# Seven block products instead of eight for two pairs of token groups: a gate projection on one core of Trainium2

## The reference

```python
def act_qdq(x):        # one scale for the whole tensor, 16 bits
    scale = max(max(abs(x)) / 32767, 1e-12)
    return clip(round(x / scale), -32768, 32767) * scale
# lpbq_dequant(w): 4-bit rounding with a scale for each block of 32 weights
x = act_qdq(layernorm(x2))
up   = act_qdq(x @ lpbq_dequant(w_up).T)      # w_up, w_gate: 1536 x 512
gate = act_qdq(x @ lpbq_dequant(w_gate).T)
gate = act_qdq(gate * fixed_qdq_u16(sigmoid(gate)))
out  = x2 + act_qdq(gate * up) @ lpbq_dequant(w_down).T
```

## Time and profile before

| | |
|---|---|
| Median of 3 runs | 889.84 us (888.32 to 889.88) |
| The profiled execution | 889.12 us, span of its instructions 887.3 us |
| TensorE matmul | 858.3 us busy, 97% of the span, 4108 matmuls |
| VectorE | 689.5 us busy, 78% |
| ScalarE | 585.5 us busy, 66% |
| GpSimd | 195.4 us busy, 22% |
| Granted TensorE clock, mean | 0.994 |

### The profile page before, as it was taken

One profiled execution on the slowest core, in us unless ns is written; L12 is line 12 of the kernel. 1 busy time (PEld: TensorE's weight loads), 2 busy tenths in 40 slices (PEclk: granted clock), 3 DMA queues, 4 the chain that ended last, 5 costly groups with the idle time before them and its releaser, 6 DMA issues.

```text
span 887.3 us, 11953 instructions
## 1 busy us (share of the span) xinstructions
PE 858.3 (97%) x4108; PEld 424.5 (48%) x4108; DVE 689.5 (78%) x965; ACT 585.5 (66%) x712; POOL 195.4 (22%) x170
## 2 busy tenths in 40 slices
PE   7999969999999999999999999999899989999998
PEld 5877544444444444444444444444444434444443
DVE  4879885566647459689998987584999997999892
ACT  2468776785655366599999987752889965455430
POOL 0099948399300295000000000000000000000000
PEclk9999989999999999999999999999999999999999
DMA  9822228766989549999779964997998887989872
GB/s 348 339 84 109 107 83 288 232 169 188 304 252 313 196 156 238 270 379 371 261 258 341 334 236 161 357 378 262 323 406 271 277 319 273 374 299 401 316 294 96
DMA packets 118402, 236.56 MB, mean 267 GB/s; under 512 B 47952, under 2 KB 57168, under 8 KB 116304
## 3 DMA queue, kind: packets, MB, share of 16 engines
q1 hardware_dynamic: 117200, 231.77, 74.0%
q10 hardware_dynamic: 1152, 4.19, 1.2%
HBM read 130.55 MB, written 95.42 MB: 255 GB/s over the span
## 4 chain that ended last, share of the span: by engine, by line
PE 71%; DVE 9%; POOL 8%; issue 6%; DMA 3%; SPq 1%; ACT 1%; DVEq 0%; ACTq 0%; POOLq 0%
PE ps L1106 28%; PE ps L1043 21%; PE ps L1159 13%; PE ps L1059 4%; PE ps L1186 4%; DVE big L1960 3%; DVE big L1953 3%; POOL big L875 2%; DMA big<-in_L_ffn_w_gate_dram 2%; POOL big L832 1%; POOL big L826 1%; PE ps L1176 1%; POOL small L872 1%; DMA big<-up_park 1%; POOL big L830 1%
## 5 line engine op out<-in xcount | busy, mean ns | idle before, releaser
L1106 PE MATMUL ps<-big 128*128 (+1 forms) x1152 | 248.8, 379 | 0.0
L1204 ACT ACTIVATE big<-ps 128x1024 f32<-128x1024 f32 (+2 forms) x154 | 126.4, 830 | 147.7 <-PE ps L1043 62.5
L1043 PE MATMUL ps<-big 128*128 (+1 forms) x864 | 186.6, 379 | 0.7 <-DVE big L1736 0.7
L1106 PEld LDWEIGHTS ps<-big 128*128 128x128 f16 x1152 | 112.7, 98 | 135.9
L1043 PEld LDWEIGHTS ps<-big 128*128 128x128 f16 x864 | 84.4, 98 | 102.7 <-issue 0.9
L1159 PE MATMUL ps<-big 128*128 128x512 f16 x576 | 125.1, 379 | 3.2 <-DVE big L1981 3.2
L817 POOL PARTITION_ALL_REDUCE small<-small x8 | 2.9, 368 | 451.6 <-DVE small L1922 170.1
L1781 DVE TENSOR_REDUCE small<-big 128x1 f32<-128x1024 f32 x36 | 43.8, 1218 | 71.0 <-ACT big L1204 71.0
L1159 PEld LDWEIGHTS ps<-big 128*128 128x128 f16 x576 | 56.2, 98 | 71.6 <-issue 2.9
L1140 PE MATMUL ps<-big 128*128 128x512 f16 x384 | 84.2, 379 | 4.3 <-ACT big L1489 4.3
L1874 DVE TENSOR_REDUCE small<-big 128x1 f32<-128x1024 f32 x48 | 58.2, 1215 | 13.7 <-ACT big L1204 13.6
(11 more groups left out here) (118 smaller groups left out, 1222.3 us busy)
## 6 DMA issues: line engine op xcount, KB each, us to landing
big<-up_park SPq DMA_DIRECT2D x90, 512.0 KB, 6.7
big<-gate_park SPq DMA_DIRECT2D x48, 512.0 KB, 6.3
up_park<-big SPq DMA_DIRECT2D x48, 512.0 KB, 4.1
gate_park<-big SPq DMA_DIRECT2D x36, 512.0 KB, 2.7
sign_park<-big SPq DMA_DIRECT2D x36, 256.0 KB, 2.7
big<-in_x_dram SPq DMA_DIRECT2D x8, 1024.0 KB, 18.5
x_park<-big SPq DMA_DIRECT2D x8, 1024.0 KB, 3.9
product_park<-big SPq DMA_DIRECT2D x16, 512.0 KB, 3.5
```

Source lines behind the costliest of these rows:

```text
L1043: mm = nc.tensor.matmul(unit_banks(n)[:, j], WG[:, x, a, k % 2, o:o + P], XT[:, g, b, k], start=(k == 0 and a + b == 0), stop=(k == KC - 1 ...
L1106: mm = nc.tensor.matmul(ps[:, b + j], WU[:, a, t // 3, k, t % 3], XT[:, g, c, k], start=(k == 0 and a + c == 0), stop=(k == KC - 1 and c = ...
L1204: return nc.scalar.activation(dst, src, ACT.Copy)
```

## The change

Groups 4 and 5 are taken as a second pair. There are 24 flat units and 12 quads; quads 0 to 5 take groups 6 and 7, quads 6 to 11 take groups 4 and 5. The differences of groups 4 and 5 are made at units 11 to 13 (and kept where the one pair's were), those of groups 6 and 7 at units 18 to 20, in another place. What lay on units 24 to 35 moves: the down weights' pieces to units 14, 16, 19 and 21, with new waits; the loads of the up weights to quads 0 and 1, behind the last store of down weights; their block maxima to quads 1 to 4, scales to quads 4 and 5; their pieces to quads 7 to 10. At the end SP fetches five gate tiles in a row, since their stores ended six quads earlier.

```diff
-FLAT_G = 6
+FLAT_G = 4
 FLAT = FLAT_G * UPG
-QUADS = UPG
+PAIRS = (NG - FLAT_G) // 2
+QUADS = PAIRS * UPG
-DOWN_AT = (14, 17, 20, 23)
-PARK_AT = (16, 19, 22, 25)
-TURN_AT = 25
-UP_AT = (0, 1, 2, 3)
-LOAD_AT = 26
-BLOCKS_AT = (28, 29)
-SCALE_AT = (30, 32)
+DOWN_AT = (14, 16, 19, 21)
+PARK_AT = (17, 19, 22, 24)
+TURN_AT = (19, 12)
+UP_AT = (7, 8, 9, 10)
...
+        def pair_group(pr):
+            return FLAT_G + 2 * (PAIRS - 1 - pr)
+
+        def turns(pr):
+            t = part(HT0 + 4 * UW, 4096) if pr else part(U0, 4096)
...
+                    if g == 6:
+                        sp.wait_ge(t_raw, T_RAW + 4)
...
+                if q == 0:
+                    park_down_weights(KC - 1)
+                if q < 2:
+                    load_up_weights(2 * q)
+                    load_up_weights(2 * q + 1)
+                if q == UP_AT[0] + 1:
+                    sp.wait_ge(q_mm, Q_MM + done_p7(UPG * (PAIRS - 1) - 1))
+                    sp.wait_ge(t_lo, T_LO + 4 * PAIRS)
...
-            fetch_late_gate(1)
-            fetch_late_gate(2)
             for x in (2, 3):
                 park_half(QUADS - 1, x)
-            fetch_late_gate(3)
-            fetch_late_gate(4)
...
+            for x in (1, 3):
+                sp.wait_ge(c_st[x], C_ST + 16 * UPG)
+            for i in range(1, 6):
                 fetch_gate(i)
...
-                    pe.wait_ge(t_lo, T_LO + 4)
+                    pe.wait_ge(t_lo, T_LO + 4 * PAIRS)
...
+                else:
+                    act.wait_ge(t_lo, T_LO + 4)
...
+                act.wait_ge(t_raw, T_RAW + (count if pr or j < 2 else 8))
+                if pr == 0 and j == 0:
+                    h_turned(act, NG - 1)
...
+                elif pr == 0:
+                    dve.wait_ge(t_lo, T_LO + 4)
+                    dve.wait_ge(wd_turned, 32)
                 if j == 0:
-                    dve.wait_ge(wd_turned, 32)
                     h_turned(dve, g)
                     h_turned(dve, g + 1)
...
+                if 1 <= q < 5:
+                    up_block_max(q - 1)
+                if q == 4:
+                    block_scales(1)
+                if q == 5:
+                    common_scale(1, 3)
                 half_max(q, 0)
```

More of the change, by code:

```diff
@@ L240, in whole_sum @@
             return part((4 + x) * 2048, 1536)
-        T = part(HT0 + 4 * UW, 4096).bitcast(F16).rearrange("p (j l k t) -> p j l k t", j=4, l=2, k=2)
+        def pair_group(pr):
+            return FLAT_G + 2 * (PAIRS - 1 - pr)
+        def turns(pr):
+            t = part(HT0 + 4 * UW, 4096) if pr else part(U0, 4096)
+            return t.bitcast(F16).rearrange("p (j l k t) -> p j l k t", j=4, l=2, k=2)
         raw_sum = part(U0 + 4096, 2048).rearrange("p (s w) -> p s w", s=2)
@@ L594, in _ @@
             fetch_gate(7)
+            for x in (2, 3):
+                park_half_sign(QUADS - 1, x)
             def next_gates(n):
@@ L1063, in first_of @@
             def first_of(q, base):
-                g = FLAT_G
-                six(base + 1, q, WG[:, 1], XT[:, g, :, 2:4], True)
+                g = pair_group(q // UPG)
+                six(base + 1, q % UPG, WG[:, 1], XT[:, g, :, 2:4], True)
             def quad(q):
-                base, g, n = 4 * ((q + 1) % 2), FLAT_G, q
+                base, pr, n = 4 * ((q + 1) % 2), q // UPG, q % UPG
+                g, T = pair_group(pr), turns(pr)
                 need(pe, c_ev, C_EV + 4 * (q - 1) if q > 1 else 0)
@@ L1361, in _ @@
                 nc.scalar.activation(sign_out[:, u % 2], gate_out[u % 3], ACT.Sign).then_inc(sign_ev, 1)
-                for j in range(4):
-                    if u == TURN_AT + j // 2:
-                        turn_hi(j)
+                for pr in range(PAIRS):
+                    for j in range(4):
+                        if u == TURN_AT[pr] + j // 2:
+                            turn_hi(pr, j)
                 if u % 2 and u < 2 * NG - 3:
@@ L1771, in turn_raw, with turn_lo @@
                                         ALU.add if j == 2 else ALU.subtract).then_inc(t_raw, 1)
-            def turn_lo(j):
-                dve.wait_ge(t_hi, T_HI + j + 1)
-                hi, lo = (T[:, j, l].rearrange("p k t -> p (k t)") for l in range(2))
+            def turn_lo(pr, j):
+                dve.wait_ge(t_hi, T_HI + (j + 1 if pr else 4 + j + 1))
+                hi, lo = (turns(pr)[:, j, l].rearrange("p k t -> p (k t)") for l in range(2))
                 nc.vector.scalar_tensor_tensor(lo, raw_sum[:, j % 2], 0.25, hi, ALU.mult,
@@ L1796, in _ @@
                     sum_lo(SUM_AT.index(u))
-                if u == TURN_AT - 1:
-                    turn_raw(0)
-                    turn_raw(1)
-                if u == TURN_AT:
-                    turn_lo(0)
-                    turn_lo(1)
-                    turn_raw(2)
-                    turn_raw(3)
-                if u == TURN_AT + 1:
-                    turn_lo(2)
-                    turn_lo(3)
-                if u in BLOCKS_AT:
-                    up_block_max(2 * BLOCKS_AT.index(u))
-                    up_block_max(2 * BLOCKS_AT.index(u) + 1)
-                if u == SCALE_AT[0]:
-                    block_scales(1)
-                if u == SCALE_AT[1]:
-                    common_scale(1, 3)
+                for pr in range(PAIRS):
+                    if u == TURN_AT[pr] - 1:
+                        turn_raw(pr, 0)
+                        turn_raw(pr, 1)
+                    if u == TURN_AT[pr]:
+                        turn_lo(pr, 0)
+                        turn_lo(pr, 1)
+                        turn_raw(pr, 2)
+                        turn_raw(pr, 3)
+                    if u == TURN_AT[pr] + 1:
+                        turn_lo(pr, 2)
+                        turn_lo(pr, 3)
                 for c in range(OC):
```

27 lines of the change are left out of this document (8 added, 19 removed).

## The result

The changed kernel takes **896.18 us** (median of 5 runs, 894.04 to 897.33); the kernel before, on the same chip, 889.88 us (5 runs, 888.32 to 890.70). The ratio is 1.0071, with a 95% interval of 1.0053 to 1.0090: 6.3 us slower, where 887.3 was forecast. The profiled execution of the changed kernel took 896.1 us, with a span of 894.3; before it was 889.12 and 887.3.

The account below looks back on a forecast made before the run. TensorE was taken to set the stage's end: -7.8 for matmuls removed, +1.1 and +2.4 flat-stage stalls, +0.3 and +1.5 hand-over, sum -2.5, giving 887.3 us by the median of 889.84. Range 883.6 to 891.6; the forecast's own 885.5 to 889.0.

Parts of the forecast that it names:

- the size of the pair's operations: Flat stage, units 11 to 13: the second pair's VectorE operations beside GpSimd take 1.5 us each, bounds 1.2 and 2.1.
- the lock rival: Flat stage: each of the second pair's eight operations waits a whole GpSimd instruction, chain 3.6 later; 890.9 us, chance 0.13.
- 0.3 for another wait: Hand-over to quads: first half store lands at 271.5, about when quad 1's first combination wants its buffer; 0.3 us lost.
- the forecast's own upper end for the flat part: Flat stage and quad 0's second product: at most 7 us lost, with the second pair's eight operations at 2.1 each.
- the hand-over's 1.5: Quad 1: combine(2, 0) ends at 283.0 behind load and block maximum, TensorE wants it at 281.6; 1.5 us, bounds 0 and 8.
- the late loads rival: Quad 1: up-weight load lands 12 us after issue, VectorE waits at up_block_max(0) before combine(1, 1); 893.7 us, chance 0.12.
- the natural pieces in quads 7 to 10: Quads 7 to 10: they cost TensorE 0.4 us as in quads 0 to 3, nothing net, bounds -0.4 and +0.8.
- GpSimd's pieces for the up weights: Late quads: all eight pieces end at about 353, quad 10 asks for the last at 355; hidden by 2 us.
- the block maxima and scales in quads 3 to 5: Quads: a 1.75 us maximum fits VectorE's 2.71 gap; quad 4's scales make combine(4, 1) 1.7 late, recovered; no cost.
- the last up transposes: End of the quads: issued in quad 11, landing at 371.9 before ScalarE's first scaling at 373; hidden by 1 us.
- the differences in units 11 to 13 take 2 us each: Sign against the forecast: with up products starting after 371, these long flat-stage operations would point to the lock rival.
- quad 1 holds the gap: Sign against the forecast: with up products starting after 371, a gap there would point to the late loads rival.

Follow-up runs that it names:

- the kernel with both causes away: Changed kernel with the third natural_hi's wait shortened, first two down-piece sets at units 15 and 17, up-weight loads 48 KB instead of 768 KB: 883.05 us.
- the run with a light GpSimd: Changed kernel with GpSimd quantizing only 2 of 24 blocks in each piece of the down weights: 889.09 us, ratio 0.9992.

## Why the prediction was wrong, step by step

**The saving was right.** Thirty-six matmuls fewer at 0.2160 are 7.8 us, and the kernel with both causes away gains 7.0.

**The step that failed first** is the size of the pair's operations: "I take 1.5". They took 2.07 each, the upper bound that the prediction had worked out (2.1) and given to the lock rival. Eight times 0.57 is 4.6, and the pair was ready 4.4 later. From there the times are 3 to 4.5 later than written: the last `turn_lo` 220.5 for 216.1, the copy of unit 20 ends at 253.9 for 250.4, that of unit 23 at 263.7 for 260.6. The chain itself was followed rightly; the gaps stand ahead of unit 23 (1.67, forecast 1.1) and of quad 0's second product (2.00, forecast 2.4). That their sizes come so near is in part luck: ScalarE was 3 us later than written, and TensorE had already lost 2.39 itself. For new is a gap ahead of unit 20 (2.39), where by the forecast's times (sign of unit 17 at 233.4, so its copy at 232.4; unit 20 wants the banks at 233.7) the cover held by 1.3; the copy ended at 236.5. The gap of 0.70 at quad 0's first combination is a wait for the store of unit 22, which stands behind one set of down transposes in SP's queue (issued from 259.32, the store at 262.87). The forecast had 0.3 for another wait, that of quad 1's first combination, which cost nothing. In all 6.8 for 3.8; the forecast's own upper end for the flat part, 7 with the eight operations at 2.1, held (6.1), and the rival's price of 3.6 more for the lock was about right, its chance of 0.13 too low. I had chosen between the two ends by one sum split of 2.20, over three `natural_lo` that said otherwise. The trace of the kernel before had two longer ones of the same form, beside GpSimd too, that I did not weigh:

```profile
181.66 3.03 DVE L1752 SCALAR_TENSOR_TENSOR big<-big 128x1536 f16<-128x1536 f32 x1
...
191.25 2.33 DVE L1752 SCALAR_TENSOR_TENSOR big<-big 128x1536 f16<-128x1536 f32 x1
```

Alone, this form takes 1.76 (in the run with a light GpSimd), so its four rows beside GpSimd in the kernel before (1.82 is the fourth) are 0.1 to 1.3 longer, 0.6 in the mean; one row was no measure.

**The second step** is the hand-over's 1.5, where 4.18 was measured, and 2.0 by the clock behind it. The load landed as it should: 275.83 was its issue for 271.7 forecast, 281.5 its landing, 5.7 after issue for 5.6. That is 4.2 later than written, and TensorE wanted `combine(2, 0)` just as much later (285.8 for 281.6), so the load by itself would have cost the 1.5. So the late loads rival, with its landing 12 us after issue, came true in its place and not by its mechanism. What I left out is the other side of the same crowd. From the end of `combine(1, 1)` to the end of `combine(2, 0)` I counted 2.6; it took 4.25, with 0.26 and 1.29 for half stores, and 0.96 for another half store stood ahead of `combine(1, 1)`. These three, 2.5 together, are the 2.7 by which the gap was longer, but for 0.2. Later maxima showed that the stores alone would have held VectorE 6.48. I had priced the load at its landing in a full queue and given the half stores behind it in the same queue no wait at all, as if they still landed after 2.6. The cause is the volume: 3 MB in two quads, on engines that stood at 0.83; with 48 KB loads the gap was gone, with one load a quad it was 1.68.

**The clock was not in the sum.** 74.55 for the 336 matmuls against 72.86 with a gap of 1.68: 1.7 us for a gap of 4 in place of one of under 2.

**Sum as measured:** -7.8 + 6.8 (flat and quad 0) + 4.2 (hand-over) + 2.0 (clock) + 0.2 and 0.8 (the last small gap, the pipeline's ends), less the 0.4 that before lost too: +5.8, beside a start of the stage 0.4 later; the forecast had -2.5.

**Right, at no price:** the natural pieces in quads 7 to 10 (0.23 lost, as before); GpSimd's pieces for the up weights, which nobody waits for; the block maxima and scales in quads 3 to 5; the up products without a gap.

**Wrong, but free:** the last up transposes were not hidden. ScalarE's first scaling starts at 383.31 behind a wait of 3.4 for them, while TensorE, which has four bank pairs of cover there, lost nothing.

The signs that the prediction named did their work: "the differences in units 11 to 13 take 2 us each" and "quad 1 holds the gap" were written as what would make it wrong, and both came about. I had weighed them as alternatives of 0.13 and 0.12, though neither excludes the other; both together, -2.5 + 3.6 (the lock's price) + 2.7 (the hand-over gap beyond 1.5) + 1.7 (the clock) = +5.5, stood in no case.

## What to carry to other kernels

Two losses in different stages add up; rivals that do not exclude one another need a case of their own for both. When work is moved next to another engine's work or into a full stretch of transfers, price it by the worst row of its kind in that company, and price what was already there again too: the small stores that free a buffer suffer more from 3 MB of loads than the loads do. Spread such loads over more of the stage before you give them another queue: one load a quad in place of two took the gap from 4.18 to 1.68, though the engines stayed full (100.7% from 260 to 300), and ScalarE's queue made it longer.

## What the runs showed that was not expected

- An operation of VectorE on two SBUF tensors of 128x1024 takes 1.2 us alone and 1.6 to 2.5 beside GpSimd's block quantization. GpSimd pays too: its pieces of the down weights ended at 236.2, against 229.5. With the pair's operations narrow they ended at 230.7, so it is VectorE's operations that hold GpSimd up.
- With the DMA engines at 98.8%, a 256 KB store lands after 7.1 us in place of 2.6; with the same loads on a second queue after 5.7, and the loads themselves then after 11.2 in place of 8.2. The share alone does not give the time: at 100.7%, with one load a quad, it is 5.5.
- A gap of 4.2 us amid dense matmuls was followed by a granted clock of 0.94 and then 0.87, one of 3.29 by 0.91 (280 to 300), and one of 1.7 us by 1.00.
